# Moving the first weighted-sum products, the copy of c and two batch loads inside a fused attention and mixture-of-experts layer

## The reference

```
xn = layernorm(x)
q, k, v = xn@Wq.T, xn@Wk.T, xn@Wv.T        # 16 heads of 32; q and k get rotary position terms
attn = softmax(causal(q @ k.T / sqrt(32)))
out  = x + (attn @ v) @ Wo.T
         + sum over the 2 chosen experts e of w_e * (xn @ expert_w[e].T + expert_b[e])
```

## Time and profile before

| | |
|---|---|
| median of 3 runs | 976.4 us (975.77 to 978.81) |
| the profiled execution | 978.25 us, its span 976.5 us |
| TensorE busy | 911.8 us (93%), mean granted clock 0.986 |
| VectorE busy | 734.4 us (75%) |
| GpSimd busy | 545.3 us (56%) |
| ScalarE busy | 434.7 us (45%) |
| chain that ended last | PE 68%, DVE 11%, DMA 7%, ACT 7% |

### The profile page before, as it was taken

One profiled execution on the slowest core, in us unless ns is written; L12 is line 12 of the kernel. 1 busy time (PEld: TensorE's weight loads), 2 busy tenths in 40 slices (PEclk: granted clock), 3 DMA queues, 4 the chain that ended last, 5 costly groups with the idle time before them and its releaser, 6 DMA issues.

```text
span 976.5 us, 18753 instructions
## 1 busy us (share of the span) xinstructions
PE 911.8 (93%) x6589; PEld 453.6 (46%) x6589; DVE 734.4 (75%) x1328; ACT 434.7 (45%) x711; POOL 545.3 (56%) x553
## 2 busy tenths in 40 slices
PE   2888898989999999989999999998999999999897
PEld 1344344444454544545555555554454444544343
DVE  7888989887989899954444444466878887788893
ACT  5357867757755443432211111123443444434442
POOL 1544677576585446663333333228777777777651
PEclk9999999999999999999999999999999999999999
DMA  6365688798787443396655555556555574466441
GB/s 245 108 227 185 169 280 289 216 318 298 196 269 286 149 159 124 118 338 199 209 175 173 173 173 173 173 184 184 164 186 177 179 228 152 145 187 184 149 131 55
DMA packets 107963, 188.63 MB, mean 193 GB/s; under 512 B 11872, under 2 KB 65248, under 8 KB 102624
## 3 DMA queue, kind: packets, MB, share of 16 engines
q1 hardware_dynamic: 97072, 152.03, 46.8%
q0 software_dynamic: 10800, 35.40, 12.7%
HBM read 117.13 MB, written 70.25 MB: 192 GB/s over the span
## 4 chain that ended last, share of the span: by engine, by line
PE 68%; DVE 11%; DMA 7%; ACT 7%; issue 4%; POOL 2%; SPq 1%; another core or an unknown queue 0%; ACTq 0%; DVEq 0%
PE psum L985 19%; PE psum L1070 12%; PE psum L1094 6%; PE psum L1033 6%; PE psum L1020 5%; PE psum L1036 5%; PE psum L1002 5%; PE psum L1079 4%; PE psum L962 3%; DVE top L1573 3%; ACT pT L783 3%; DMA c_rows<-c_turn 2%; DMA w_rows<-w_hl 2%; PE psum L1004 2%; ACT x_in L716 1%
## 5 line engine op out<-in xcount | busy, mean ns | idle before, releaser
L783 ACT ACTIVATE pT<-psum,factors 128x512 f32<-128x512 f32 (+1 forms) x352 | 219.0, 641 | 247.4 <-PE psum L1020 227.4
L1573 DVE TENSOR_REDUCE top<-psum 128x1 f32<-128x384 f32 (+3 forms) x352 | 210.2, 636 | 26.6 <-PE psum L1004 25.8
L1070 PE MATMUL psum<-xT,w_att 128*128 128x512 f16 x768 | 197.6, 383 | 7.6 <-DVE xT L1524 5.0
L985 PE MATMUL psum<-w_exp,x_gT 128*128 x852 | 195.3, 379 | 0.7 <-DVE x_gT L1529 0.6
L1020 PE MATMUL psum<-q_stack,k_stack 98*128 98x256 f16 (+3 forms) x512 | 128.3, 303 | 16.7 <-ACT pT L783 13.0
L613 POOL DMA_INDIRECT x_g<-xn_rows,tok_of x71 | 67.1, 945 | 131.9 <-PE psum L962 129.3
L1002 PE MATMUL psum<-k_stack,q_stack 96*128 96x384 f16 (+3 forms) x512 | 126.8, 301 | 12.6 <-DVE top L1573 9.6
L1529 DVE TENSOR_TENSOR x_gT<-psum,x_gT 128x512 f16<-128x512 f32 x71 | 49.0, 692 | 103.8 <-ACT x_gT L807 83.3
L985 PEld LDWEIGHTS psum<-w_exp,x_gT 128*128 128x128 f16 x852 | 83.4, 98 | 85.8 <-issue 1.2
L807 ACT ACTIVATE x_gT<-psum 128x512 f16<-128x512 f32 x71 | 42.3, 597 | 169.9 <-PE psum L962 167.3
L597 POOL TENSOR_SCALAR_AFFINE_SELECT pT<-pT 128x512 f32<-128x512 f32 x128 | 98.4, 780 | 20.9 <-ACT pT L783 20.9
(11 more groups left out here) (176 smaller groups left out, 1276.7 us busy)
## 6 DMA issues: line engine op xcount, KB each, us to landing
y_rows<-y_sb SPq DMA_DIRECT2D x71, 256.0 KB
w_in<-w_all SPq DMA_DIRECT2D x12, 1024.0 KB, 12.5
q_stack<-qk_rows SPq DMA_DIRECT2D x96, 128.0 KB
k_stack<-qk_rows SPq DMA_DIRECT2D x96, 128.0 KB
x_in<-x SPq DMA_DIRECT2D x8, 1024.0 KB, 11.1
qk_rows<-q_hl SPq DMA_DIRECT2D x32, 256.0 KB
qk_rows<-k_hl SPq DMA_DIRECT2D x32, 256.0 KB
xn_rows<-x_in SPq DMA_DIRECT2D x8, 1024.0 KB, 5.4
```

Source lines behind the costliest of these rows:

```text
L783: act.activation(p_of(j, h, heads), banks[BANK_T + (NT_ * n + k) % 2][:, 0:W], ACT.Exp, scale=factors[:, 0:1]).then_inc(exp_done, 1)
L985: now = pe.matmul(banks[s % 4], x_gT[s % 4][:, xp * C + c, :], w_exp[:, bass.ds(e, 1), wp, c, :].rearrange("p e d -> p (e d)"), start=n == ...
L1070: now = pe.matmul(bank, w_att[:, what, wp, c, g * P:(g + 1) * P], xT[b % 2][:, xp * C + c, :], start=at_pass == 0, stop=at_pass == 3 * C - 1)
L1573: return dve.tensor_reduce(out=top[:, h:h + heads, i], in_=banks[BANK_S + k % 2][:, 0:heads * W].rearrange("p (h t) -> p h t", h=heads), a ...
```

## The change

In steps 1 to 15 TensorE does `times_v(n - 1, 0)` and `(n - 1, 1)` after the first half of the q projection instead of at the end of the step before; step 15 keeps its own at its end. `turn_c` goes behind `shifted_scores(n, 10)` in all these steps, in step 15 behind `times_v(15, 1)`, and ScalarE's `copy_c` goes behind `exps(n, 9)` (step 15: `exps(n, 10)`). `split_c` loses one operation. Batch 3 is asked for in step 5 instead of 6, batch 4 in step 12 instead of 10. The second gather is issued right behind the first. The last part of `times_v_last` goes ahead of the 9 passes.

```diff
-    TAKE_AT = {4: 2, 6: 3, 10: 4}
+    TAKE_AT = {4: 2, 5: 3, 12: 4}
...
                     gather_x(0)
+                    gather_x(1)
...
-                if n == N1 - 1:
-                    gather_x(1)
...
                 exps(n, 8)
-                if n < N1:
-                    copy_c(n + 1)
                 if n + 3 < N:
                     high_qk(1, n + 3)
                 exps(n, 9)
-                if N1 <= n < N - 1:
+                if n < N - 1 and n != N1 - 1:
                     copy_c(n + 1)
                 exps(n, 10)
+                if n == N1 - 1:
+                    copy_c(n + 1)
...
                     project_qk(0, n + 3, 0, 6)
+                if 0 < n < N1:
+                    times_v(n - 1, 0)
+                    times_v(n - 1, 1)
...
-                if n < N1:
-                    turn_c(n + 1)
                 shifted_scores(n, 9)
                 if wo:
                     project_out(wo[0], BANK_KO, 4, 8)
                 shifted_scores(n, 10)
-                if n < N1:
+                if n == N1 - 1:
                     times_v(n, 0)
                     times_v(n, 1)
-                elif nxt:
+                if nxt:
                     turn_c(n + 1)
-                else:
+                elif not nxt:
                     times_v_last(0, 1, 2)
...
             times_v_last(1, 0, 2)
+            times_v_last(1, 2, 4)
             pe.wait_ge(o_last, 1)
             project_out(N - 1, OUT_LAST[J - 1], 0, 9)
-            times_v_last(1, 2, 4)
...
-                dve.tensor_tensor(c_f[:], tops, c_scale[:], ALU.mult)
                 own.link(dve.tensor_tensor(c_hl[:, 0, :], tops, c_scale[:], ALU.mult))
-                dve.tensor_tensor(c_hl[:, 1, :], c_f[:], c_hl[:, 0, :], ALU.subtract).then_inc(c_made, 1)
+                dve.scalar_tensor_tensor(c_hl[:, 1, :], tops, 2.0 ** -LOG_C, c_hl[:, 0, :], ALU.mult, ALU.subtract).then_inc(c_made, 1)
```

More of the change, by code:

```diff
@@ L125, in moe_attention_layer @@
     c_scale = at("c_scale", [P, HG * J], F32)
-    c_f = at("c_f", [P, HG * J], F32)
     c_wide = at("c_wide", [P, P], F16)
```

## The result

| | before | after |
|---|---|---|
| median of 12 runs | 975.45 us | 980.86 us |
| ratio of the two, 95% interval | | 1.0051 (1.0033 to 1.0069) |
| the profiled execution | 978.25 us, span 976.5 | 980.71 us, span 979.0 |
| TensorE busy, mean granted clock | 911.8 us, 0.986 | 913.3 us, 0.985 |
| VectorE busy | 734.4 us | 732.8 us |

The kernel became slower by 5.4 us, or 0.5%; 979.6 had been predicted, 973.2 to 983.4 as the range. So medians decide on the size, and the traces on the places.

What follows compares the result with a forecast made beforehand. Late steps were taken as bound by TensorE, steps 0 to 15 by its waits for ScalarE, VectorE and transfers. Terms summed to +3.4, taken as 3.2: 979.6 us against the 976.4 median, range 973.2 to 983.4.

Steps and rivals of the forecast that it cites:

- The three places of the move: Steps 11, 13 and 14: new waits of TensorE cost +1.6, +4.1 and +2.7, clock falls +1.6 and +1.1.
- Four places have such work: List of places where work between the products' old and new position waits for another engine, losing 3.14 us of cover.
- rival B: Steps 1, 4, 13, 14: VectorE gets scores earlier, TensorE's 7.5 us of waits for it go; 972.1 us, chance 0.15.
- I price a fall of the clock at 1.6: Taken from step 6: 3.9 us at granted clock 0.56 behind a 3.35 us wait lose some 1.6 us.
- priced at +1.1: Step 14: two waits, together 2.7 us, may let the clock fall; two thirds of 1.6, bounds 0 and 1.6.
- The loads: Moved batch loads shorten waits: -0.95 in step 6 (bounds 0 and -2.6), -0.85 in step 10.
- The gathers and the bias: Step 15: the wait and clock fall won are 4.2; 0.6 taken off for experts' first tiles, leaving -3.6.
- The operation less: split_c: one VectorE operation less is worth 0.25 in steps 13 and 14, elsewhere 0.
- The end: Last part of the products no longer waits for 9 passes, so normalisation and last sums come sooner: -2.0.
- A: Rival: the clock does not fall behind the waits of steps 13 and 14; 977.1 us, chance 0.24.
- C: Rival: moved loads win their full price, 2.6 in step 6, no transfer of c taking it up; 978.0 us, chance 0.10.
- D: Rival: later copy_c holds SP's queue, and full queues of steps 3 to 10 pass it on; 983.6 us, chance 0.11.

Runs made afterwards that it cites:

- b_part: Changed kernel with the move of the first products undone in steps 11, 13 and 14 alone; ratio 0.9951 to the kernel before.
- b_early_c: Changed kernel with turn_c and copy_c back in their old places in steps 0 to 14, products in their new one; ratio 1.0004 to the kernel before.
- b_none: Changed kernel with the whole move of steps 0 to 14 undone; 973.33 against 977.64 us for the kernel before, ratio 0.9954.
- a_move: Kernel before with only the move of the first products, turn_c and copy_c in steps 0 to 14; 989.82 against 976.09 us, ratio 1.0138.
- c_no15: Changed kernel with step 15's part undone; ratio 1.0071 to the kernel before.
- d_warm: Changed kernel with added matmuls filling TensorE's waits, 16 ahead of scores(15, 1) and 6 ahead of ranks; ratio 1.0064 to the kernel before.
- a_loads: Kernel before with only the two batch loads moved, to steps 5 and 12; 975.28 against 976.09 us, ratio 1.0001.
- d_best: b_none with added matmuls ahead of shifted_scores units 9 and 10 of steps 1 to 3 and unit 9 of step 6; 971.73 against 976.57 us, ratio 0.9936.
- a_end: Kernel before with only the last part of times_v_last put ahead of the nine passes; ratio 0.9982.
- d_split: Kernel before with only the one operation less in split_c; ratio 0.9975.
- d_no15: Kernel before with the two loads, the end and the operation less, nothing moved in any step; 969.95 against 976.57 us, ratio 0.9934.
- a_step15: Kernel before with only step 15's part: turn_c behind the products, copy_c behind the last exponentials, second gather right behind the first; ratio 1.0034.

## Why the prediction was right where it was, and where not

The prediction was right in its sign, in most of its mechanism and nearly in its size: 3.2 us against 5.4. It was partly luck. Place by place in the table, steps 12 to 15 cost 13.2 us where 11.1 were forecast, the steps up to 11 gained 2.7 where 2.1 were, and steps 18 to 31, for which there was no term, took off another 2.0.

**The three places of the move.** Step 11: TensorE waits 1.56 us for `chosen` (1.6 predicted). Start of step 14: 4.42 for `c_turn` (4.4). Step 14's end: 1.19 for the comparisons and 1.52 for `c_turn`, +3.0 us in all (2.7 and 1.1). These four waits were worked out from the timeline alone, and b_part shows that nearly all of the move's price lies in these steps, to within some 2.4 us. The step that failed is "Four places have such work": the list left out the projection of q, which waits for VectorE's sum of step 13's second output projection. The late copy covered it, so the sum came out near, but the cause was half wrong: 4.4 of the 7 us come without the late copy (b_early_c). Of rival B's 7.5 us of waits for VectorE 5.2 are still there in the kernel after, the three of steps 13 and 14 in full (1.44, 1.28, 1.49). The wait of step 1 is 0.64 instead of 0.95 wherever the move is made; those of step 4 are gone in b_none too, where it is not, and scatter.

**The clock.** "I price a fall of the clock at 1.6" was right as a unit: the falls of the kernel before add up to 1.7 each, and so does the row it was taken from (3.9 x 0.44). Three things were mis-sized. The fall behind the 4.42 us wait is twice as long, 3.4 us, of which 2.8 fall on work. A fall behind the wait for `chosen` was not counted; it is there in the kernel after and in b_early_c (1.7 us) and not in a_move and c_no15, with waits of 1.56 to 1.73 us in all four. And in step 6 the clock was counted when waits grew but not when one shrank. The two waits of step 14, priced at +1.1, let nothing fall. The section HAM oscillation of TensorE: Matmul & The Clock Gate in the Trainium skill has the clock throttled again by waits that are longer than the bursts between them, a condition that the prediction left out. The trace agrees behind 4.42 us, and by d_warm it is the standing still that does it there. The two waits of 1.19 and 1.52 are short beside the work around them, and the clock stayed, though it fell behind the wait of 1.56 for `chosen`.

**The loads.** -0.95 was predicted for step 6; the trace has -3.2: the wait went from 3.35 to 1.41, as the store landed in 7.3 us instead of 11.1, and the fall of 1.7 is gone. With the loads alone the wait is 2.76 and the fall stays, so this execution flatters them. (The forecast's own sum for this term, 2.6 less 1.2 and 0.2, gives 1.2 as it is written and not 1.6; 1.6 comes out when the 0.2 is added.) Over all traces, steps 6 to 8 stand at -0.6 to -4.2 with the loads moved and at -1.1 to +1.0 without. For step 10, -0.85 was predicted from a wait that is anything from nothing to 4.03 us in executions of the same code; in all nine kernels with the loads moved the columns 9-11 stand between -0.2 and -0.5, in the others between 0 and +4.6. Alone they gave nothing that can be measured (a_loads). That their worth lies in the executions in which step 10 waits long is likely, but not shown.

**Step 15.** -3.6 predicted, -3.4 in the trace up to the first tile. "The gathers and the bias ... are not earlier by as much; I take off 0.6 (bounds 0 and 2)" is the term that was mis-sized. The bias is what the traces point to. The first wait in the expert stage is for the rows of the fifth tile. SP's load of the biases (2048 KB), GpSimd's fifth gather and TensorE's row for that tile, in the kernel before:

```profile
432.93 0.36 SPq L523 DMA_DIRECT2D bias_all<-bias  x1
437.05 0.96 POOL L613 DMA_INDIRECT x_g<-xn_rows,tok_of  x1
441.56 0.60 PE L962 MATMUL psum<-ident,x_g 128*128 128x128 f32 x4
```

and in the kernel after, where TensorE's row is the one with the wait of 1.34 us, at 449.81:

```profile
441.62 0.36 SPq L522 DMA_DIRECT2D bias_all<-bias  x1
443.65 0.96 POOL L612 DMA_INDIRECT x_g<-xn_rows,tok_of  x1
```

The first product of the experts is 7.09 us later than before (439.65 against 432.56), the gather only 6.60, but the load 8.69. Where TensorE waits for this gather, in ten kernels, the load was issued 0.6 to 2.8 us ahead of the gather, and TensorE takes up the tile 7.9 to 8.3 us after the load's issue (9.3 in d_warm, 9.7 in d_best). Where the profile gives the load's landing (7.6, 7.8, 7.9 and 9.3 us), the wait ends 0.2 to 0.6 us behind it. In the four kernels without such a wait (before, a_loads, a_end, a_move) the load is 3.7 to 4.1 us ahead, and TensorE needs the rows only 8.2 to 8.6 after its issue. So the gather seems to land with the load; no run moved the load, and it is not shown by an experiment.

From the first product to the end of the last, the expert stage costs +1.5 us in the kernel after, +1.3 to +5.9 in the six others with step 15's part, and +1.8 to +2.0 in c_no15, d_split and d_no15, which do not have it but have the operation less, and whose first tile also comes 2.1 to 2.6 us sooner. In the three others it is within 0.2 us of before. The rest of the column "tiles" is steps 16 and 17, -2.1 to +1.6: the kernel before has a fall of the clock there at 676 us and the kernel after has none, which makes its -0.6. Up to the first tile and the expert stage together, the seven kernels with the part stand at -2.2 to +2.9, the three with the operation less alone at -0.3 to -0.6. Whether the part wins or loses is not settled: +3.3 alone, +2 between d_no15 and b_none, -2 between c_no15 and the changed kernel.

**The operation less.** "It lies beside TensorE's work except where VectorE is behind; the 0.25 above are its worth in steps 13 and 14, elsewhere 0" failed: alone it gives 2.4 us, and up to the first tile its trace shows 2.6 in step 15. In this change most of it overlaps with step 15's part. SBUF — State Buffer of the Trainium skill, SBUF: two separate sides, has a VectorE operation with two SBUF inputs held for a whole GpSimd instruction that reads SBUF; the trace agrees that it is held, for two such instructions in a row where the section speaks of one, and shows what follows: with three operations two were held (2.64 and 1.21 us), with two only one (2.63).

**The end.** -2.0 predicted, -2.0 in the trace, -1.8 alone. Steps 18 to 31 stand at -2.0 in the kernel after, a place for which there was no term: 1.7 of it is a fall of the clock in the kernel before that the kernel after does not have (below).

**Parts and whole.** The whole costs 7.3 us less than its parts (7.7 by its ratio of 1.0051). The intervals of the six ratios together, taken as independent, leave some 5 us to either side of that, an estimate from their half-widths. Two places of the table hold most of it: in steps 6 to 8 loads and move stand at -1.1 and +1.0 alone and at -3.2 together, and in the tiles step 15's part costs 2.8 alone and nothing in the kernel after, 1.3 of it in the expert stage and 2.1 by the fall in step 17. Both are columns that scatter, so this is where to look, not a cause that is shown.

**The rivals.** A is refuted for step 13, right for step 14. C's price was exceeded in step 6 of this execution (-3.2 for -2.6), by the clock that it left out, but not with the loads alone (-1.1). D has no place in the traces: columns 9-11 are at most 0.4 from before.

## What to carry to other kernels

Work moved out of the time ahead of a wait must be laid beside every wait of the whole stretch that it is taken from, also those that lie at zero now because two engines arrive together: a bank that is summed late is such a one. Test an order step by step; here the same move costs nothing in 12 steps and 10 us in three. A wait that is taken away just ahead of a stage that is fed by transfers is won only if all of these come earlier as well. Here every kernel that reached the first tile 2 us or more sooner waited there for rows. The four kernels with the loads, the end and the operation less that undo the move in steps 11, 13 and 14 beat both kernels (0.9934 to 0.9954), and their intervals overlap. The simplest of them moves nothing: the two loads, the end and the operation less, at 0.9934 of the kernel before.

## What the runs showed of the hardware

Over the 14 traces a fall of the clock costs 1.7 us or twice that. It is twice behind the waits of 4.42, 4.51 and 4.64 us at the start of step 14, and in step 6 behind 3.49 (a_step15) and 3.98 (a_move). It is once behind 3.35 (before) and, in step 10 of a_step15, behind 4.03. So the length of the wait alone does not decide. In step 17 two waits of about 1.5 and 1.83 us cost twice 1.7 in d_no15, b_part, b_early_c and d_best, once in b_none and nothing in d_warm. Whether the clock falls at all behind a wait of 1 to 2 us changes between executions. Behind the wait of 1.16 us in step 29, in the kernel before, windows of 2 us:

```profile
915.00:917.00 2.00, 2.00 (x14) 0.54 (x16) 2.00 (x3) 0.00 (x0) 1.97 (x4) 0.62 0.75 221
917.00:919.00 2.00, 2.00 (x16) 0.65 (x12) 1.51 (x2) 0.00 (x0) 1.00 (x1) 0.53 0.83 249
```

and behind the same wait in the kernel after:

```profile
919.84 0.39 PE L1000 MATMUL psum<-k_stack,q_stack 96*128 96x256 f16 x2 [1.16 <-ACT c_turn L788]
...
921.00:923.00 2.00, 1.87 (x18) 0.66 (x22) 2.00 (x4) 0.00 (x0) 1.97 (x3) 1.00 0.66 164
923.00:925.00 2.00, 2.00 (x23) 0.66 (x16) 1.96 (x2) 0.00 (x0) 1.47 (x2) 1.00 0.80 264
```

That is 1.7 us of span. VectorE has one operation less in these steps of the kernel after, but in a_loads, whose code from step 13 on is that of the kernel before, the clock did not fall there either. It fell in before, a_end, a_move and a_step15 and in none of the other ten, so that a part of the change in it is not ruled out. The executions of one kernel scatter along the clock: the six of a_move go from 986.5 us at a mean clock of 0.988 to 992.8 at 0.978. What decides whether the clock falls behind such a wait stayed open.
